# Row sums of P, row maxima, variances and the exp factor of an attention and feed-forward block: which engine does them

## What is computed

```python
def reference(x, Wq, bq, ..., W, b, logits, u):
    x = x + layernorm(attention(layernorm(x)))        # Wq, Wk, Wv, Wp and biases
    x = x + layernorm(layernorm(x) @ W[idx] + b[idx]) # idx: argmax of log_softmax(logits) + gumbel(u)
    return x

att = q @ k.T / sqrt(32)                              # per batch and head
att = where(mask == 0, -inf, att)
y = softmax(att) @ v
```

## Time and profile before

| | |
|---|---|
| median of the runs shown | 2315.77 us |
| span of the profiled execution, first to last instruction | 2314.4 us |
| its time against the median | 1.4 us less, by the span; no other time of it is given |
| TensorE busy | 2226.8 us (96%) |
| VectorE busy | 1712.2 us (74%) |
| GpSimd busy | 1703.5 us (74%) |
| ScalarE busy | 1558.7 us (67%) |
| mean granted TensorE clock | 0.991 |
| DMA, mean | 59 GB/s |

### The profile page before, as it was taken

The page is one execution under the profiler, slowest core; times in us unless marked ns, Lnnn a source line. Parts: engine busy times, 40 slices in busy tenths (PEclk is TensorE's granted clock), DMA queues, the critical chain, the costliest instruction groups (busy, mean ns, idle before and its releaser), DMA issues.

```text
span 2314.4 us, 42414 instructions
## 1 busy us (share of the span) xinstructions
PE 2226.8 (96%) x14484; PEld 932.2 (40%) x14484; DVE 1712.2 (74%) x4758; ACT 1558.7 (67%) x2822; POOL 1703.5 (74%) x1563
## 2 busy tenths in 40 slices
PE   4899999999999999999999999999999999999997
PEld 2444433433444443343344444343344444334322
DVE  7978776876477878687368878778728787768876
ACT  7657667677755767667864766767776576675673
POOL 3248699789735879978962769988983486997852
PEclk9999999999999999999999999999999999999998
DMA  7213122112233213112132413111124231211101
GB/s 214 69 35 89 36 56 64 36 29 82 55 93 75 59 41 70 39 35 59 48 92 59 100 31 80 45 34 43 45 60 103 68 78 34 60 46 49 27 1 37
DMA packets 222818, 137.42 MB, mean 59 GB/s; under 512 B 145194, under 2 KB 195082, under 8 KB 222602
## 3 DMA queue, kind: packets, MB, share of 16 engines
q1 hardware_dynamic: 222310, 134.65, 23.5%
q10 hardware_dynamic: 292, 0.07, 0.0%
HBM read 39.69 MB, written 16.78 MB: 24 GB/s over the span
## 4 chain that ended last, share of the span: by engine, by line
PE 74%; DVE 9%; issue 6%; POOL 5%; ACT 4%; DMA 2%; SPq 0%; POOLq 0%; ACTq 0%; DVEq 0%
PE acc L1310 13%; PE acc L1346 13%; PE acc L1330 12%; PE acc L1281 9%; PE acc L1282 9%; PE acc L1283 9%; PE acc L1361 5%; POOL P L845 3%; ACT P L960 3%; DVE MP L1065 2%; PE acc L1334 2%; DVE acc L1061 2%; DVE STA L1016 1%; PE acc L1286 1%; PE acc L1318 1%
## 5 line engine op out<-in xcount | busy, mean ns | idle before, releaser
L960 ACT ACTIVATE P<-acc,EX 128x512 f32<-128x512 f32 (+2 forms) x1920 | 1084.5, 637 | 421.8 <-PE acc L1330 204.0
L845 POOL TENSOR_TENSOR P<-P 128x512 f32<-128x512 f32 x982 | 1219.4, 1277 | 65.1 <-PE acc L1346 51.3
L1065 DVE TENSOR_REDUCE MP<-acc 128x1 f32<-128x512 f32 (+1 forms) x1088 | 718.4, 679 | 172.2 <-PE acc L1310 169.4
L1310 PE MATMUL acc<-KST,QST 96*128 96x512 f16 (+10 forms) x2112 | 596.0, 334 | 24.7 <-DVE MP L1065 8.1
L1330 PE MATMUL acc<-QST,KST 98*128 98x512 f16 (+2 forms) x1920 | 589.2, 355 | 13.5 <-ACT P L960 6.6
L1061 DVE CUSTOM_DVE_ANT_0 acc<-acc,CB 128x96 f32<-128x96 f32 (+7 forms) x1024 | 450.3, 455 | 189.0 <-PE acc L1310 186.6
L1346 PE MATMUL acc<-P,V 128*32 128x512 f32 (+2 forms) x3840 | 430.6, 545 | 1.4 <-ACT P L960 0.9
L1310 PEld LDWEIGHTS acc<-KST,QST 96*128 96x128 f16 x2112 | 192.8, 97 | 364.7 <-issue 62.6
L1330 PEld LDWEIGHTS acc<-QST,KST 98*128 98x128 f16 x1920 | 183.2, 97 | 280.5 <-ACT P L960 69.5
L824 POOL TENSOR_TENSOR RR<-RR,NHALF 128x1 f32<-128x1 f32 x256 | 140.9, 555 | 185.8 <-DVE RR L1022 105.0
L836 POOL TENSOR_TENSOR QKL<-SC,QKH 128x384 f16<-128x384 f32 (+1 forms) x128 | 134.3, 1049 | 123.5 <-ACT QKH L935 123.4
(11 more groups left out here) (152 smaller groups left out, 2506.2 us busy)
## 6 DMA issues: line engine op xcount, KB each, us to landing
QST<-QKH SPq DMA_DIRECT2D x128, 128.0 KB, 3.2
XR<-in_L_attn_x_dram SPq DMA_DIRECT2D x60, 256.0 KB, 2.9
out_dram<-XR SPq DMA_DIRECT2D x60, 256.0 KB, 2.2
KST<-QKH SPq DMA_DIRECT2D x128, 96.0 KB, 2.6
XB<-in_L_attn_x_dram SPq DMA_DIRECT2D x48, 252.0 KB
QST<-QKL SPq DMA_DIRECT2D x64, 128.0 KB, 3.3
KST<-QKL SPq DMA_DIRECT2D x64, 96.0 KB, 2.7
XB<-in_L_attn_x_dram SPq DMA_DIRECT2D x20, 256.0 KB, 3.2
```

Of the source, the lines that this page charges most:

```text
L845: e.tensor_tensor(P[:, acc, a, :], P[:, acc, a, :], P[:, buf, a, :], ALU.add).then_inc(g_s, 1)
L960: e.activation(P[:, p_buf[u, g, sb_], a, t0:512], bank(*step)[:, t0:512], ACT.Exp, scale=EX[:, 1:2]).then_inc(a_e, 1)
L1065: e.tensor_reduce(maxima(u, g)[:, r, a, ci:ci + 1], bank(*s)[:, 0:n], AX.X, ALU.max).then_inc(v_m, 1)
L1310: i = e.matmul(bank(*s)[:, 0:n], QST[0:96, h, 128 * r:128 * r + 128], KST[0:96, h, c0:c0 + n], start=True, stop=True)
```

## The change

1. The narrow blocks of P are no longer summed by `sum` on TensorE: VectorE adds both into the group's first buffer, four heads in one instruction, in all groups but the last. In units with j = 0 the first buffer now serves as "acc" too. TensorE's "acc" sum is then the last of the group, behind the adds.
2. Whole blocks are added two heads an instruction. Blocks 3 and 6 of units with j = 2 and 3 and 7 of units with j = 3 are added by VectorE, the others by GpSimd. By the instruction lists GpSimd has 371 such adds (before: 982 of one head), VectorE 141 of two heads (before: 42 of one head) and 126 narrow ones.
3. `MHL` becomes 128 wide; SP transposes it with a DMA into `MROW` (`turn_m`), and the TensorE transposes, their identity and ScalarE's copy are gone.
4. The variance of the projections' results comes from ScalarE: Square with an accumulated output into `SQ`, and one small VectorE instruction. 128 of these.
5. `exp` takes its factor from a register, loaded once.
6. `rstd` of the first normalisation is done for four row blocks at once, in all units but the first.
7. The planner's durations follow (`EXP`, the adds), and with them all queues are laid out anew. `MASK` is off, `PATIENCE` is 0.

```diff
-def sum_blocks(j):
-
-    return [s for s in range(j > 0, 3 * j + 1) if on_pe(j, s)] + (["acc"] if j else []) + [3 * j + 1, 3 * j + 2]
+    EXP = 0.833, 93
+    MASK, NARROW, SQUARE, BATCH, QUADS = False, True, True, True, 2
+    ONPE = (0, 4, 7, 8)
+    ADDED_BY_DVE = ((2, 3), (2, 6), (3, 3), (3, 7))
+    def added(self, u, g):
+        j = u % self.NJ
+        whole = [s for s in range(1, 3 * j + 1) if not self.on_pe(u, g, s)]
+        return whole + [3 * j + 1, 3 * j + 2] * self.narrow_added(u, g)
+    def adders(self, u, g, sb):
+        j = u % self.NJ
+        if sb > 3 * j:
+            return [("dve", 0, 4)]
+        if u == self.NU - 1 and g > 1:
+            return [("gp", 0, 2), ("dve", 2, 2)] if g == 2 else [("dve", 0, 2), ("dve", 2, 2)]
+        if (j, sb) in self.ADDED_BY_DVE:
+            return [("dve", 0, 2), ("dve", 2, 2)]
+        return [("gp", a, self.QUADS) for a in range(0, 4, self.QUADS)]
...
-        self.add("dve", rank, 1060, ("stats", k, u, r), after)
+        if k % 2 and self.SQUARE:
+            self.add("act", rank, 690, ("square", k, u, r), after)
+            self.add("dve", rank, 130, ("stats", k, u, r), [("act", "square", k, u, r)])
...
-            add("pe", s - 0.2, 300, ("shift", u, g), [("dve", "peaks", u, g)])
-            add("act", s - 0.2, 480, ("shift", u, g), [("pe", "shift", u, g)], [("MROW", ("sp", "shift", u, g))])
-            add("sp", s - 0.2, 1300, ("shift", u, g), [("act", "shift", u, g)]
+            add("sp", s - 0.2, 1250, ("turn_m", u, g), [("dve", "peaks", u, g)], [("MROW", ("sp", "shift", u, g))])
+            add("sp", s - 0.2, 1300, ("shift", u, g), [("sp", "turn_m", u, g)]
...
+                elif kind == "turn_m":
+                    u, g = s[1:]
+                    n = 4 * u + g
+                    sp.wait_ge(v_m, DV["peaks", u, g])
+                    if n:
+                        sp.wait_ge(d_m[(n - 1) % 4], 32 * ((n - 1) // 4 + 1))
+                    e.dma_start_transpose(MROW[:, :].rearrange("p (o n) -> p o n", o=1), MHL[:, n % 2, :]).then_inc(d_h, 16)
...
-                    e.tensor_tensor(P[:, acc, a, :], P[:, acc, a, :], P[:, buf, a, :], ALU.add).then_inc(g_s, 1)
+                    e.tensor_tensor(P[:, acc, h, :], P[:, acc, h, :], P[:, buf, h, :], ALU.add).then_inc(g_s, 1)
...
+                elif kind == "square":
+                    k, u, r = s[1:]
+                    job = ("p" if k == 1 else "f", u, r)
+                    ac.wait_ge(p_w, PE["proj", job, 3])
+                    e.activation(VOID[:, :], bank("proj", job, 0), ACT.Square, accum_out=SQ[:, k // 2, r:r + 1]).then_inc(a_s, 1)
...
                     e.activation(P[:, p_buf[u, g, sb_], a, t0:512], bank(*step)[:, t0:512], ACT.Exp,
-                                 scale=EX[:, 1:2]).then_inc(a_e, 1)
+                                 scale=factor).then_inc(a_e, 1)
...
+                    e.tensor_tensor(P[:, acc, h, t0:512], P[:, acc, h, t0:512], P[:, buf, h, t0:512], ALU.add).then_inc(v_s, 1)
```

More of the change, by code:

```diff
@@ L21, in most_chunks, with width @@
     return max(len(chunks(384 * j + 96 * (r + 1))) for r in range(4))
[L24 to L31 removed]
+def width(j, sb):
+    return (512, 512, 344, 176)[max(sb - 3 * j + 1, 0)]
 def p_blocks(NB, NJ):
@@ L278, in attend @@
                     [] if sb else [("psO", ("dve", "out", u, g))])
-            before = []
[L280 to L285, removed]
+                if sb in self.added(u, g):
+                    i = self.added(u, g).index(sb)
+                    for who, a0, n in self.adders(u, g, sb):
+                        before = [("pe", "pv", u, g, 0)]
+                        if masked and self.MASK and not j:
+                            before.append(("dve", "mask", u, g, 0))
+                        if i:
+                            was = self.added(u, g)[i - 1]
+                            before = [(self.adder_on(u, g, was, a), *self.adder(u, g, was, a)) for a in range(a0, a0 + n)]
+                        done = [("dve", "mask", u, g, sb)] if masked and self.MASK else [("act", "exp", u, g, sb, a) for a in range(a0, a0 + n)]
+                        add(who, at, 142 + 2.12 * n * w if who == "gp" else 100 + 1.04 * n * w, ("add", u, g, sb, a0), done + before)
@@ new lines, in attend @@
+            before = []
+            for sb in blocks:
+                w = 512 if sb == "acc" else width(j, sb)
+                if sb == "acc":
+                    was = self.added(u, g)[-1]
+                    done = [(self.adder_on(u, g, was, a), *self.adder(u, g, was, a)) for a in range(4)]
+                    at = 3 * j if 3 * j + 1 in blocks else last
+                else:
+                    done = [("dve", "mask", u, g, sb)] if sb >= 3 * j and self.MASK else [("act", "exp", u, g, sb, a) for a in range(4)]
+                    at = sb
+                add("pe", s + at / (last + 1) + 0.02, 1.65 * w + 60, ("sum", u, g, sb), done + before,
@@ L294, in attend @@
-            add("dve", s + 0.95, 1600, ("invert", u, g), [("pe", "sum", u, g, last)]
+            add("dve", s + 0.95, 1600, ("invert", u, g), before
                 + [("dve", "out", *divmod(s - 1, 4))] * (s > 0))
@@ L678, in summed, with made, scaled, turned_m @@
         def summed(u, g, sb_, a):
-            step = ("add", u, g, sb_, a)
-            return (v_s, DV[step]) if order.adder(u, g, a) == "dve" else (g_s, GP[step])
+            step = order.adder(u, g, sb_, a)
+            return (v_s, DV[step]) if order.adder_on(u, g, sb_, a) == "dve" else (g_s, GP[step])
+        def made(u, g, sb_, a0=0, n=4):
+            if order.masked_by_dve(u, g, sb_):
+                return v_k, DV["mask", u, g, sb_]
+            return a_e, max(AC["exp", u, g, sb_, a] for a in range(a0, a0 + n))
+        def scaled(k, u, r):
+            return g_ln, GP["rstd", k, u, order.batch(k, u, r)[0]]
+        def turned_m(u, g):
+            return d_h, 16 * (m_slot[u, g] + 1)
         def normed(k, u, r):
@@ L707, in valued @@
             return max(AC["evac", ("v", u, a)] for a in range(3))
-        def exped(u, g, sb_):
-            return max(AC["exp", u, g, sb_, a] for a in range(4))
         block = ctx.enter_context(nc.Block())
@@ L853, in _ @@
             ac = Lean(e)
+            factor = None
             for s in order.act:
@@ L1087, in _ @@
                     dv.wait_ge(p_pv, PE["pv", u, g, 0])
-                    at = added(u % NJ).index(sb_)
+                    at = order.added(u, g).index(sb_)
                     if at:
-                        dv.wait_ge(*summed(u, g, added(u % NJ)[at - 1], a))
-                    e.tensor_tensor(P[:, acc, a, :], P[:, acc, a, :], P[:, buf, a, :], ALU.add).then_inc(v_s, 1)
+                        for a in range(a0, a0 + n):
+                            dv.wait_ge(*summed(u, g, order.added(u, g)[at - 1], a))
@@ L1312, in _ @@
                     i.then_inc(p_m, 1)
-                elif kind == "shift":
-                    u, g = s[1:]
-                    half = bank("peaks", u, g)[0:8, 0:256].bitcast(F16)
-                    pe.wait_ge(v_m, DV["peaks", u, g])
-                    for r in range(4):
-                        i = e.transpose(half[:, 128 * r:128 * r + 128],
-                                        MHL[:, (4 * u + g) % 2, r, :, :].rearrange("p l a -> p (l a)"), IDH[:, :])
-                    i.then_inc(p_m, 1)
                 elif kind == "score":
@@ L1330, in _ @@
                     i = e.matmul(bank(*s)[:, t0:512], KST[0:98, h, 128 * sb_:128 * sb_ + 128], QST[0:98, h, t0:512],
-                                 start=True, stop=dg < 0)
-                    if dg >= 0:
+                                 start=True, stop=dg < 0 or order.MASK)
+                    if dg >= 0 and not order.MASK:
                         pe.wait_ge(d_cb, 16)
```

252 lines of the change are left out of this document (148 added, 104 removed).

## The result

The changed kernel takes 2390.23 us (median; 2380.01 to 2391.51), 1.031 of the kernel before, with a 95% interval of 1.029 to 1.033. The forecast was 2250, the range 2200 to 2298: wrong in sign. Rival C, VectorE's turns with GpSimd, had 0.08.

A forecast was written before the change was run, and what follows sets the result against it. TensorE's own work was taken as the bound over nine tenths of the program. 2314.4 - 55 - 20 - 5 - 10 + 25 = 2249 us span, given as 2250, range 2200 to 2298.

The forecast's parts named there:

- Rival C: VectorE becomes the bound over the whole program, slower than before, from 1.38 us mean wait per add; chance 0.08.
- Bound, TensorE's savings: TensorE's own work bounds nine tenths of the program; narrow sums save 55 us, transposes 20, shorter exps 5.
- GpSimd's 10: 240 single adds moved off GpSimd give TensorE back 10 us where GpSimd was full, between 0 and 33.
- VectorE's price: VectorE's extra adds and waits for GpSimd cost TensorE 25 us, between 0 and 70.
- The count of the sums: TensorE would show 98 sums of 512, 784 instructions, and no narrow form beyond the last group's.
- Transposes of the maxima by DMA: DMA replacing TensorE's transposes costs 0, covered by SP's long waits; uncovered in every group it would cost 192 us.
- ScalarE: Exps 60 ns shorter, 1920 times, 115 us less on ScalarE; worth 5 us to TensorE, between 0 and 35.
- The small instruction stays: On VectorE, bn_stats and half of bn_aggr go, 112 us less; the variances' small instruction remains.
- VectorE, turns: VectorE's 267 adds meet GpSimd's with chance 0.62 and wait 1.2 us each, 200 us; VectorE busy 2100 us.
- my signs of 1.6 and 2.3: VectorE's narrow adds of 4 x 344 take 1.6 us in the mean undisturbed, 2.3 or more with turns.
- What this costs TensorE: VectorE's extra 386 us, 8.8 us in 50, overfills seven or eight crowded slices at 3 us: 25 us, 0 to 70.
- Rival B: VectorE lags in more stretches because the plan lacks the turns; late peaks stop TensorE, 70 us, 2295 total; chance 0.19.

The follow-up runs named there:

- h1_no_turns: The change, its order kept, with VectorE's adds as reduces of one SBUF input and the small variance instruction as tensor_scalar: 2238.49 us, 0.968 of the kernel before.
- e10_reg: The kernel before, its order unchanged, with only the exp factor put in a register: 2308.01 us, ratio 0.996.
- f1_scalar: The change, its order kept, with the small variance instruction as tensor_scalar instead of scalar_tensor_tensor: 2379.78 us, 1.029 of the kernel before.
- e1_reduce: The change, its order and waits kept, with each of VectorE's 267 adds made a reduce of one SBUF input: 2253.38 us, 0.973 of the kernel before.
- e4_none: The change with narrow sums back on TensorE and whole blocks outside the last unit on GpSimd in pairs, planned anew: 2331.97 us, 1.006 of the kernel before.
- g1_costs: The change with the small variance instruction as tensor_scalar, laid out anew with longer add durations for the turns in the plan: 2340.69 us, 1.011 of the kernel before.

## Why the prediction was wrong

- **Bound, TensorE's savings.** Right in sum. Without turns (h1_no_turns) the change is 76 us faster than before, where the sum has 55 + 20 + 5 + 10 = 90 without VectorE's price. No run takes the 55, the 20 or GpSimd's 10 alone. The count of the sums was off: 96 of 512 rows and the last group's two narrow ones, 784 instructions together.
- **Transposes of the maxima by DMA.** Right at 0. The new transpose lands in 2.3 us. In the change TensorE's matmuls wait 1.4 us in all for `MROW`'s DMAs:

```profile
PE acc L1438 <- DMA QST<-MROW: 1.4, 2, 1.1
```

- **ScalarE.** The pointer operand was priced at 60 ns by a copy from SBUF; it is 94 (694 to 600 in e10_reg). The Trainium skill's 93 (ScalarE: Activation LUTs, What ACT_TABLE_LOAD costs) was the better price. A factor in a register costs nothing of it: the 94 ns are gone with it. On the path it gave 8 us for my 5.
- **The small instruction of the variances.** "The small instruction stays" was false: its form changed, to two SBUF inputs, and so it takes turns too. In the change's order this cost 10 to 15 us (f1_scalar; h1_no_turns against e1_reduce), and 38 us in the order of e4_none. I read what the line computes and not which of its operands are tensors.
- **VectorE, turns.** The mechanism was read rightly from the last unit, and its size not badly: I put 200 us on the adds. Undisturbed they would take 141 x 1.21, 63 x 1.59 and 63 x 0.88 us, 326 us, by the means of those that met no GpSimd instruction (the reduces of h1_no_turns take as much); they took 460.4, so 134. The chance was right, 162 of 267 or 0.61 for my 0.62; the wait was 0.83 us for my 1.2. With the small instruction's 26 that makes 160. VectorE's busy time came to 2012 where I said 2100, and the adds of 4 x 344 to 1.80 us in the mean, between my signs of 1.6 and 2.3.
- **"What this costs TensorE"** is the step that failed: 25 us, between 0 and 70. Without this term the sum gives 2226 us, so 164 would have been needed. I spread VectorE's extra work evenly over windows of 50 us and let only what exceeds a window count. Measured, the turns cost 137 us for the adds (e1_reduce) and 152 with the small instruction (h1_no_turns), nearly as much as VectorE was delayed, 134 and 160. Three things were left out. A turn is not work that could be moved: it falls into a queue of fixed order, in front of peaks that TensorE is about to need (its matmuls wait 88 us for them instead of 19), and what TensorE then idles is gone, even if VectorE rests later. The turns also delay GpSimd (its pairs 2458 ns for 2361, all its work 1444 us for 1341), and its adds and VectorE's both hold P's buffers. And the kernel whose TensorE idles more was granted the lower clock, up to 37 us of it. That the cost comes so near to VectorE's own delay is in part chance, for GpSimd's delay and the clock are in it too.
- **Rival C** had the mechanism and the sign, but its condition was false: it wanted VectorE full, 1.38 us a turn. It came with 0.5 us a turn (134/267) and VectorE 84% busy. By asking for a full engine I gave it 0.08. Rival B told the way better, with peaks that come late and a TensorE that stops, but priced it at 70 us. Its cause, a plan that doesn't know of the turns, is only part: in g1_costs the plan knows their mean, and 39 us come back.

By TensorE's own account the 152 us between the change and h1_no_turns are 98 us more of idle time (190 for 92) and 54 us more of busy time for the same matmuls. Of the 98, 69 ended with a maximum from VectorE, 13 with an add of VectorE's and 10 with an exp; of the 54, up to 37 are the clock. What stays open: what lies behind each of these. A late exp or a late maximum can itself come from a buffer that was held too long, and no run took one of the waits or the clock away alone.

## What to carry to other kernels

Before work with two SBUF operands goes to VectorE beside a busy GpSimd, count its instructions, not its microseconds: each can wait for the rest of the GpSimd instruction that is running, and now and then for those behind it, even if it has one column; a one-column tensor_scalar with a pointer in place of the scalar_tensor_tensor was free of that here. In program orders fixed ahead, price a delay that the plan doesn't know at its full length, and do not set it off against idle time: here 134 us of it cost 137, and 160 cost 152, with the engine at 84%. Of the narrow adds, only those where GpSimd doesn't add (units with j = 0) paid, 8 us; the turns' durations in the plan gave another 14.

## What the runs showed of the hardware

Of the adds and small instructions with two SBUF inputs, those that meet a long GpSimd instruction mostly end after it by about their own time: 1.96 us for one column, where 0.15 us is usual, and 1.08 us after it for an add of 1.21 us. Now and then they wait for several, up to 6.43 us for one column in e4_none. GpSimd's pairs wait too: 3.44 us at most, where 2.36 is usual. Reduces, also from SBUF, and tensor_scalar of one column show none of it (1213 and 206 ns in the mean in h1_no_turns; the 128 tensor_scalars lie between 198 and 215 ns, though 47 of them began while GpSimd worked):

```profile
L1209 DVE TENSOR_REDUCE JUNK<-P 128x2 f32<-128x1024 f32 x141 | 169.7, 1213 | 41.0 <-POOL P L947 37.0 <-ACT P L1069 3.5
L1117 DVE TENSOR_SCALAR RR<-SQ,EC 128x1 f32<-128x1 f32 x128 | 26.3, 206 | 20.5 <-ACT VOID L1048 20.4
```

TensorE's granted clock between 100 and 2200 us was 1.00 in the kernel before and in h1_no_turns, and 0.98 in the change, which has the same matmuls as h1_no_turns but a TensorE that idles 190 us over the span instead of 92: 17 stretches at 1.2 GHz, the one shown right behind a wait of 2.8 us.
